# Last turn with transposes by TensorE, and an epilogue with matmuls in TensorE's pauses: a cross-attention and quantized feed-forward kernel on one core

## The chip, the cores and the metric

One Trainium2 chip, one NeuronCore. The metric is the device time of one execution in microseconds (us), the median of several runs. The profile is of one further execution; its times are counted from the start of its span.

## What is computed

Two blocks on x, 32 batches of 100 tokens and 256 features, with a context of 361 tokens per batch. The reference, cut to what matters:

```
x = x + xattn(layernorm(x), ctx, ctx, WQ, WK, WV, WO, mask)
x = x + ffn(layernorm(x), W1, b1, W2, b2)

def xattn(Q, K, V, ...):                     # 16 heads of 64
    logits = Qh @ Kh.T / sqrt(64) + mask * -1e9
    return concat(softmax(logits) @ Vh) @ WO

def ffn(x, ...):                             # 256 -> 1024 -> 256
    h = gelu(qlinear(x, W1, b1))
    return qlinear(h, W2, b2)

def qlinear(x, W, b):
    amin, amax = min(x), max(x)              # over the whole tensor
    scale = max((amax - amin) / 255, 1e-8)
    zp = clip(round(-amin / scale) - 128, -128, 127)
    xq = clip(round(x / scale) + zp, -128, 127)
    wq, sw = symmetric codes of W, -127 .. 127
    return ((xq - zp) @ wq.T) * (scale * sw) + b
```

The range of each quantized input is taken over all batches, so the first matmul of the feed-forward block can't begin before the last batch is through attention, and the second not before every hidden value is known.

## The kernel before, in words

**Stages.** A first stage (to about 105 us) computes the queries of all batches. Then a loop over the batches does attention: one partial turn in front ("first"), 31 turns of a hardware loop ("whole"), one partial turn behind it ("last"), which finishes batch 31 alone. An epilogue follows: the range of the normalized y, its codes, the first matmul with GELU, the range of the hidden values, their codes, the second matmul and the output.

**Float pairs.** Attention is done in pairs of 16-bit floats, a high and a low half. A product of two pairs is three matmuls (`split3`, lines 337 to 343).

**What a turn does for a head.** K, V and QP are the projections and the scores. MAX (VectorE, line 939) reads the scores out of PSUM into `prob` with the row's extreme, EXP (ScalarE, line 711) makes the exponential. The high half of `prob` goes into `hl` by HA on ScalarE (line 717) or, for the heads in VH = 2, 5, 8, 11, 14, by HV on VectorE (line 946). LO on GpSimd (line 585) writes the low half. DT on SP (line 484) transposes the halves of two heads into `pT` with one DMA transpose. PV (TensorE, line 1226) is nine small matmuls per head with the values, into `obank`; a column of ones beside the values gives the sum of each row.

**What it does for a group of four heads.** NORM (VectorE, lines 950 and 953) divides. AH (ScalarE, line 731) and AL (GpSimd, line 589) write the high and low halves into `ahl`. AD on SP (line 488) transposes two groups into `attT` with a DMA transpose. WO (TensorE, twelve matmuls of lines 341 to 343) is one half of the output product, and the same name on VectorE (line 986) adds it to x1, which lies in `q_all`.

**Layer norm of a batch.** LN 0 and 1 (VectorE, lines 998 and 1000) are the moments, RSTD (GpSimd, lines 593 to 597) the factor and shift, YN (ScalarE, line 734) writes y of 100 x 256, LN 2 and 3 (lines 1003, 1005) take its largest and smallest values, LN 4 (line 1007) puts them into `red`. M (line 568) copies a scale.

**Order.** Each engine's order in a turn is computed in `turn` from tables of due times (`PE_STEPS`, `ACT_STEPS`, `DVE_STEPS`, `SP_STEPS`, `POOL_STEPS`), and each engine goes through its list strictly in order. For the last turn `turn` keeps the steps that belong to the current batch. Before the change the lists of the last turn are, for TensorE, PV 6 to 15, WO 0, WO 1; for GpSimd, LO 10 to 15, AL 0, M, AL 1 to 3, RSTD; for ScalarE, HA 7, EXP 11, EXP 12, AH 0, EXP 13, HA 8, EXP 14, HA 9, EXP 15, HA 10, AH 1 to 3, YN (HA 7 to 10 are heads 10, 12, 13 and 15); for VectorE, NORM 1, MAX 15, HV 4 (head 14), NORM 2, NORM 3, WO 0, WO 1, LN 0 to 4; for SP, X, DT 5 to 7, AD 0, AD 1, OUT.

**Buffers.** `pT` and `hl` have 8 places. In PSUM, `proj` are two banks for K, V and WO, `ring` four banks for the scores of four heads, `obank` two for PV.

**Epilogue.** `top_red` (line 1249) transposes `red` by two matmuls, so that each row sees the range over all partitions; `quant_scalars` on VectorE (lines 1023 to 1031) is a chain of eight small steps, each waiting for the one before. `y_codes` (lines 1039 and 1043) and line 767 of ScalarE make codes of y for blocks of four batches; GpSimd makes those of blocks 4 to 7 (lines 632, 634). `y_transposes` (line 1258) transposes a block by eight transposes, sixteen for two blocks, into PSUM; `y_out` copies it out (line 1049 on VectorE for block 0, line 771 on ScalarE for the others). The first matmul (line 1280) does two blocks at once, four matmuls of 400 columns for each of 32 pieces of 128 hidden units, GELU is line 780, and VectorE takes the extremes of each 1600 columns of hidden values (lines 1059, 1060). Then come `top_red(1)`, the scalars again, the hidden codes (line 787 on ScalarE, lines 1078 and 1068 on VectorE) and the second matmul (line 1291), eight matmuls of 256 columns for each of 25 blocks of 128 tokens; block n waits for the codes of its chunk of 400 tokens. Line 1073 adds, and SP writes out.

Of the kernel before, what the change touches and what calls it, by code (L numbers as in the profile page):

```python
# [148 lines left out]
EARLY, LATER = slice(0, 3), slice(3, None)  # L149

S1, INV1, LO1, HI1, S2, INV2, LO2, HI2, SPAN, ZP = range(10)
SW, INVW = 10, 12
# [3 lines left out]
def build(nc, x, ctxT, mask, wq, wk, wv, wo, w1T, b1, w2T, b2, out):  # L156
# [34 lines left out]
    nmax = place("nmax", [P, H], F32)  # L191
    row = place("row", [P, 12], F32)
    red = place("red", [P, 2, 2], F32)
# [127 lines left out]
    s_ad = [sem(f"s_ad{n}") for n in range(2)]  # L321
    s_wp, s_x1 = sem("s_wp"), sem("s_x1")

    s_w12 = [sem("s_w1"), sem("s_w2")]
# [102 lines left out]
    def y_copied(eng, c):  # L427

        eng.wait_ge(*((s_yT, 1) if c == 0 else (s_yTa, c)))

# [19 lines left out]
    def _(sp):  # L450
# [26 lines left out]
        def sp_turn(b, part, steps=slice(None), dummy=False):  # L477
            for kind, n, later in turn(SP_STEPS, part)[steps]:
# [41 lines left out]
    def _(pool):  # L520
# [39 lines left out]
        def pool_turn(b, part, steps=slice(None)):  # L560
            for kind, n, later in turn(POOL_STEPS, part)[steps]:
                a = b + later
# [83 lines left out]
    def _(act):  # L646
# [58 lines left out]
        def act_turn(b, part, steps=slice(None)):  # L705
            banks = bank_of(part)
            for kind, n, later in turn(ACT_STEPS, part)[steps]:
                a, ps = b + later, banks.get((kind, n))
# [19 lines left out]
                elif kind == "AH":  # L728
                    wait(act, s_nrm, NG * a + n + 1)
                    wait(act, s_wp, 2 * a + n // 2 - 1)  # L730
                    act.activation(ahl[0:T, n, 0, :], att[0:T, n % 2, :], ACT.Copy).then_inc(s_ah, 1)  # L731
                elif kind == "YN":
                    wait(act, s_rl, 3 * a + 3)
# [58 lines left out]
    def _(dve):  # L792
# [136 lines left out]
        def dve_turn(b, part):  # L929
            banks = bank_of(part)  # L930
            for kind, n, later in turn(DVE_STEPS, part):
                a, ps = b + later, banks.get((kind, n))
# [9 lines left out]
                elif kind == "HV":  # L942
                    h = VH[n]
                    wait(dve, s_exp, H * a + h + 1)
                    wait(dve, s_pv, H * a + h // 2 * 2 + 1 - RT)
                    dve.tensor_copy(hl[0:T, h % RT, 0, 0:S], prob[0:T, h % RP, 0:S]).then_inc(s_hv, 1)  # L946
                elif kind == "NORM":
                    o = obank[n % 2][0:T, 0:GH * DV].rearrange("p (h d) -> p h d", h=GH)
# [67 lines left out]
        link = chain(dve, s_dve)  # L1016
        wait(dve, s_ln, LN_STEPS * B)
        dve.sem_inc(s_rd, 1)
# [84 lines left out]
    def _(pe):  # L1103
# [69 lines left out]
        def pe_turn(b, part):  # L1173
            jobs, banks = turn(JOBS, part), bank_of(part)

            before = [(kind, n, later - 1) for kind, n, later in turn(JOBS, "whole")[-2:]]
            for kind, n, later in turn(PE_STEPS, part):
                a, ps = b + later, banks.get((kind, n))
# [36 lines left out]
                elif kind == "PV":  # L1215
                    j, half = n // GH, n // HT
                    pe.wait_ge(s_dt[n % RT // 2], 16 * (H // RT * a + n // RT + 1))
                    if n % GH == 0:
# [21 lines left out]
        with pe.Fori(0, B - 1) as b:  # L1240
            pe_turn(b, "whole")
        pe_turn(B - 1, "last")


# [7 lines left out]
        def y_transposes(c):  # L1252
# [7 lines left out]
            ins.then_inc(s_yt, 1)  # L1260

        top_red(0)
        pe.wait_ge(s_wq, 2)
        y_transposes(0)
        y_transposes(1)
        for pair in range(NP2):
            for m in range(NF):
                g = pair * NF + m
                if m == 2 and pair < NP2 - 1:
                    y_transposes(2 * pair + 2)  # L1270
                    y_transposes(2 * pair + 3)
                if m == 0:
                    y_copied(pe, 2 * pair)
                    y_copied(pe, 2 * pair + 1)
                if g >= 3:
                    pe.wait_ge(s_ge, g - 2)
                for k in range(KD):
                    for n in range(2):
                        c = 2 * pair + n
                        ins = pe.matmul(wide[g % 3][:, n, 0:TW], w1q[:, k, m * P:(m + 1) * P],  # L1280
                                        yT[:, k, c * TW:(c + 1) * TW], start=k == 0, stop=k == KD - 1)
                ins.then_inc(s_f1, 1)
        top_red(1)
        pe.wait_ge(s_wq, 4)
        for n in range(NT):
# [39 lines left out]
```

## Time and profile before

| | us |
|---|---|
| runs, median (lowest to highest) | 1129.66 (1129.05 to 1130.61) |
| the profiled execution, its own time | 1126.18 |
| its span | 1124.1 |
| TensorE matmuls busy | 1018.1 (91%) |
| VectorE busy | 978.2 (87%) |
| ScalarE busy | 865.1 (77%) |
| GpSimd busy | 770.6 (69%) |

The shares are means over the span. The loop over the batches covers it from about 105 to 1004 us; the last turn goes from there to about 1028, the first quantized matmul with its ranges to 1094, the second to 1124. In the profile PE is TensorE's matmuls, PEld its weight loads, DVE VectorE, ACT ScalarE, POOL GpSimd, SP the engine that issues DMAs; PEq, DVEq and so on are their sequencers.

### The profile page before, as it was taken

Reading aid. Unit: us, or ns where it says so; the run is one execution under the profiler, and the core shown is the slowest. Engines: PE = TensorE matmul, PEld = TensorE weight load, DVE = VectorE, ACT = ScalarE, POOL = GpSimd, SP = SyncE. Lnnn points to the kernel's source line nnn. Section 1 sums busy time; section 2 is a strip of 40 time slices with the busy share of each in tenths; the row PEclk is TensorE's granted clock in tenths of the full one; section 3 lists DMA queues with packets and bytes.
Section 4 is the critical chain, followed back from the end, with each engine's and each line's share of the span. In section 5 each row is a group of like instructions: output and inputs, shape, how many; then the busy total and the mean of one; then the engine's idle time right before and its main releaser. Section 6 shows DMA issues by size and latency. Waiting matters only on the chain.

```text
span 1124.1 us, 37431 instructions
## 1 busy us (share of the span) xinstructions
PE 1018.1 (91%) x10489; PEld 643.3 (57%) x10489; DVE 978.2 (87%) x2528; ACT 865.1 (77%) x1805; POOL 770.6 (69%) x1108
## 2 busy tenths in 40 slices
PE   3999999999999999999999999999999999985808
PEld 2555566666666666666666666666666666653307
DVE  5777999999999999999999999999999999973997
ACT  4555888888888888888888888888888888873916
POOL 2246877777777777777777777777777777773700
PEclk9999999999999999999999999999999999996969
DMA  8301665555555555555555555555555555555003
GB/s 253 113 1 31 130 134 131 131 135 135 135 135 131 130 135 132 130 131 134 135 135 135 135 135 135 132 130 130 134 135 135 132 130 130 134 132 153 1 0 117
DMA packets 441419, 138.22 MB, mean 123 GB/s; under 512 B 413650, under 2 KB 440374, under 8 KB 441398
## 3 DMA queue, kind: packets, MB, share of 16 engines
q1 hardware_dynamic: 441398, 137.96, 51.0%
q8 instruction: 11, 0.18, 0.1%
q14 instruction: 10, 0.08, 0.0%
HBM read 28.60 MB, written 6.55 MB: 31 GB/s over the span
## 4 chain that ended last, share of the span: by engine, by line
PE 75%; DVE 10%; ACT 5%; issue 4%; POOL 3%; DMA 1%; DVEq 1%; ACTq 0%; SPq 0%; POOLq 0%
PE front L341 19%; PE front L343 17%; PE front L342 17%; PE back L1226 8%; PE front L1208 6%; PE tp L1208 5%; POOL hl L585 3%; DVE hrange L1059 2%; DVE hrange L1060 2%; DVE prob L939 2%; ACT prob L711 2%; DVE k_l L959 1%; ACT q_h L749 1%; PE front L1291 1%; ACT ctx_h L745 1%
## 5 line engine op out<-in xcount | busy, mean ns | idle before, releaser
L585 POOL TENSOR_TENSOR hl<-prob,hl 100x361 f16<-100x361 f32 x512 | 432.1, 853 | 97.2 <-DVE hl L946 50.9
L711 ACT ACTIVATE prob<-prob,nmax 100x361 f32<-100x361 f32 x512 | 293.9, 587 | 47.7 <-DVE nmax L939 47.5
L341 PE MATMUL front<-ctx_h,wk_h 128*128 128x362 f16 x512 | 164.2, 321 | 31.3 <-POOL ctx_l L574 17.8
L1226 PEld LDWEIGHTS back<-v,pT 128*128 128x128 f16 (+1 forms) x4608 | 165.1, 98 | 45.1 <-issue 9.6
L717 ACT ACTIVATE hl<-prob 100x361 f16<-100x361 f32 x352 | 176.0, 500 | 7.9
L1226 PE MATMUL back<-v,pT 128*128 128x65 f16 (+1 forms) x4608 | 174.2, 194 | 6.3 <-DMA pT<-hl 6.2
L343 PE MATMUL front<-ctx_h,wk_l 128*128 128x362 f16 x512 | 161.7, 316 | 0.0
L342 PE MATMUL front<-ctx_l,wk_h 128*128 128x362 f16 x512 | 161.5, 315 | 0.0
L721 ACT ACTIVATE k_h<-front 128x362 f16<-128x362 f32 x256 | 118.9, 464 | 54.7 <-PE front L343 54.7
L959 DVE SCALAR_TENSOR_TENSOR k_l<-front,k_h 128x362 f16<-128x362 f32 x256 | 135.2, 528 | 24.4 <-ACT k_h L721 21.8
L939 DVE CUSTOM_DVE_ANT_0 prob<-front,mask_g,ngain 100x361 f32<-100x361 f32 x256 | 149.6, 584 | 2.2
L965 DVE SCALAR_TENSOR_TENSOR v<-front,v 128x512 f16<-128x512 f32 (+1 forms) x192 | 132.8, 692 | 20.1 <-ACT v L725 17.0
L939 DVE CUSTOM_DVE_ANT_0 prob<-tp,mask_g,ngain 100x361 f32<-100x361 f32 x256 | 147.2, 585 | 3.1
L725 ACT ACTIVATE v<-front 128x512 f16<-128x512 f32 (+1 forms) x192 | 114.3, 596 | 45.9 <-PE front L343 41.8
L341 PE MATMUL front<-wv_h,ctx_h 128*128 128x512 f16 (+1 forms) x384 | 145.9, 380 | 0.0
L342 PE MATMUL front<-wv_l,ctx_h 128*128 128x512 f16 (+1 forms) x384 | 145.5, 379 | 0.0
L343 PE MATMUL front<-wv_h,ctx_l 128*128 128x512 f16 (+1 forms) x384 | 145.5, 379 | 0.0
L946 DVE CAST hl<-prob 100x361 f16<-100x361 f32 x160 | 131.5, 822 | 0.3 <-ACT prob L711 0.3
L589 POOL TENSOR_TENSOR ahl<-att,ahl 100x256 f16<-100x256 f32 x128 | 84.5, 670 | 31.3 <-ACT ahl L731 31.3
L341 PEld LDWEIGHTS front<-ctx_h,wk_h 128*128 128x128 f16 x512 | 49.6, 97 | 88.1 <-DVE k_l L959 27.9
L574 POOL TENSOR_TENSOR ctx_l<-ctx_raw,ctx_h 128x361 f16<-128x361 f32 x64 | 53.1, 853 | 43.9 <-ACT ctx_h L745 43.9
L341 PE MATMUL front<-wo_h,attT 128*100 128x256 f16 x256 | 71.6, 280 | 2.3 <-DMA attT<-ahl 2.3
(180 smaller groups left out, 1980.8 us busy)
## 6 DMA issues: line engine op xcount, KB each, us to landing
ctx_raw<-ctxT SPq DMA_DIRECT2D x33, 361.0 KB, 3.1
pT<-hl SPq DMA_TRANSPOSE x256, 3.1
xs<-x SPq DMA_DIRECT2D x8, 400.0 KB
q_all<-x SPq DMA_DIRECT2D x32, 100.0 KB
out<-q_all SPq DMA_DIRECT2D x32, 100.0 KB
xb<-out SPq DMA_DIRECT2D x5, 640.0 KB, 7.5
out<-xb SPq DMA_DIRECT2D x25, 128.0 KB, 1.8
q_all<-wq SPq DMA_DIRECT2D x1, 1024.0 KB, 6.6
```

The lines of the kernel that those rows point to most:

```text
L341: eng.matmul(dst, lh, rh, start=first, stop=False)
L342: eng.matmul(dst, lh, rl, start=False, stop=False)
L343: return eng.matmul(dst, ll, rh, start=False, stop=final)
L585: pool.tensor_tensor(hl[0:T, n % RT, 1, 0:S], prob[0:T, n % RP, 0:S], hl[0:T, n % RT, 0, 0:S], ALU.subtract).then_inc(s_lo, 1)
L711: act.activation(prob[0:T, n % RP, 0:S], prob[0:T, n % RP, 0:S], ACT.Exp, bias=nmax[0:T, n:n + 1], scale=-1.0).then_inc(s_exp, 1)
L717: act.activation(hl[0:T, h % RT, 0, 0:S], prob[0:T, h % RP, 0:S], ACT.Copy).then_inc(s_ha, 1)
L939: dve.tensor_tensor_reduce(prob[0:T, n % RP, 0:S], ring[n % RP][0:T, 0:S], mask_g[0:T, 0:S], ngain[0:T, 0:1], 3.0e38, ALU.add, ALU.min, nm ...
L946: dve.tensor_copy(hl[0:T, h % RT, 0, 0:S], prob[0:T, h % RP, 0:S]).then_inc(s_hv, 1)
L959: dve.scalar_tensor_tensor(out=k_l[:, n % 4, :], in0=ps[:, 0:SE], scalar=KS, in1=k_h[:, n % 4, :], op0=ALU.mult, op1=ALU.subtract).then_in ...
L965: dve.scalar_tensor_tensor(out=v[:, 1], in0=ps[0:rows_of(n), :].rearrange("p (h d) -> p h d", h=HT), scalar=VS, in1=v[:, 0], op0=ALU.mult, ...
L1208: ins = pe.matmul(ring[(2 * n + h) % RP][:, 0:SE], qs[rows[h], n, :], ks[rows[h], n % 4, :], start=t == 0, stop=t == 2)
L1226: ins = pe.matmul(obank[j % 2][:, n % GH * DV:(n % GH + 1) * DV], pT[0:r, n % RT, part_ * ST + st, :], v2[half][0:r, st, v, n % HT, :], st ...
```

## The change

For the last turn, lists written out by hand take the place of those from the due times. Heads 10 to 15 and all four groups of the last batch are transposed by TensorE (PT, six per head; AT, four per group) into PSUM and copied out (PC, AC) by ScalarE or VectorE, in place of the DMA transposes DT 5 to 7 and AD 0 and 1. Two low halves move from GpSimd to VectorE (DL for head 14, DAL for group 3). Three groups of six matmuls whose results nobody reads (KW) stand between the transposes. The products come in another order (AT 0 before PV 14, AT 1 and WO 0 before AT 2 and 3), and M stands before LO 11. In the last batch the extremes are taken of x1 (LX), and the two of them are scaled and shifted (YM) to give those of y (LM). In the epilogue TensorE does matmuls without a use (`keep_warm`) while it waits, VectorE instead of ScalarE copies block 1 of the transposed codes, and the first piece of the first matmul does block 0 before block 1.

The diff, cut to its core (declarations of semaphores, `row` with two more columns, and the loops' one changed name are left out):

```diff
+LAST_PE = [("PV", n) for n in range(6, 10)] + [
+    ("PT", 10), ("KW", 0), ("PT", 11), ("KW", 1), ("PT", 12), ("KW", 2), ("PT", 13), ("PT", 14), ("PV", 10), ("PV", 11),
+    ("PT", 15), ("PV", 12), ("PV", 13), ("AT", 0), ("PV", 14), ("PV", 15), ("AT", 1), ("WO", 0),
+    ("AT", 2), ("AT", 3), ("WO", 1)]
+LAST_ACT = [
+    ("HA", 7), ("EXP", 11), ("EXP", 12), ("AH", 0), ("EXP", 13), ("HA", 8), ("EXP", 14), ("HA", 9), ("EXP", 15),
+    ("HA", 10), ("PC", 11), ("PC", 13), ("AH", 1), ("AC", 0), ("AH", 2), ("AC", 1), ("AH", 3), ("YM", 0), ("YN", 0)]
+LAST_DVE = [
+    ("NORM", 1), ("MAX", 15), ("HV", 4), ("PC", 10), ("DL", 14), ("PC", 12), ("PC", 14), ("PC", 15),
+    ("NORM", 2), ("NORM", 3), ("DAL", 3), ("AC", 2), ("AC", 3), ("WO", 0), ("WO", 1), ("LN", 0), ("LN", 1),
+    ("LX", 0), ("LX", 1), ("LM", 0), ("LM", 1)]
+LAST_SP = [("X", 0), ("OUT", 0)]
+LAST_POOL = [
+    ("LO", 10), ("M", 0), ("LO", 11), ("LO", 12), ("LO", 13), ("LO", 15), ("AL", 0), ("AL", 1), ("AL", 2), ("RSTD", 0)]
...
+    last_bank = {n: (proj[n % 2] if n < 12 else ring[n % RP]).bitcast(F16) for n in range(10, H)}
+    att_bank = [ring[n].bitcast(F16) for n in range(NG)]
...
-        eng.wait_ge(*((s_yT, 1) if c == 0 else (s_yTa, c)))
+        eng.wait_ge(*((s_yT, c + 1) if c < 2 else (s_yTa, c - 1)))
...
+                elif kind == "PC":
+                    act.wait_ge(s_pt, n - 9)
+                    wait(act, s_pv, H * a + n + 1 - RT)
+                    act.activation(pT[:, n % RT, :, 0:T],
+                                   last_bank[n][:, 0:2 * ST * T].rearrange("p (c t) -> p c t", c=2 * ST),
+                                   ACT.Copy).then_inc(s_pca, 1)
...
+                elif kind == "YM":
+                    wait(act, s_rl, 3 * a + 3)
+                    wait(act, s_ln, LN_STEPS * a + 4)
+                    act.activation(row[0:T, 12:14], row[0:T, 10:12], ACT.Identity, scale=row[0:T, 9:10],
+                                   bias=row[0:T, 8:9]).then_inc(s_ym, 1)
...
-        y_out(1)
         act.wait_ge(s_yd, 2)
...
+                elif kind == "DL":
+                    wait(dve, s_hv, len(VH) * a + VH.index(n) + 1)
+                    dve.tensor_tensor(hl[0:T, n % RT, 1, 0:S], prob[0:T, n % RP, 0:S], hl[0:T, n % RT, 0, 0:S],
+                                      ALU.subtract).then_inc(s_dl, 1)
...
+                elif kind == "LX":
+                    wait(dve, s_x1, 2 * a + 2)
+                    dve.tensor_reduce(row[0:T, 10 + n:11 + n], x1_slot(a), AX.X, (ALU.max, ALU.min)[n]).then_inc(s_ln, 1)
...
         y_out(0)
+        y_out(1)
         y_codes(2)
...
+                elif kind == "PT":
+                    if n < 12:
+                        wait(pe, s_v, 2 * ST * (a + 1))
+                    if n == 14:
+                        pe.wait_ge(s_dl, 1)
+                    else:
+                        wait(pe, s_lo, H * a + n + 1 - int(n > 14))
+                    for c in range(2 * ST):
+                        ins = pe.transpose(last_bank[n][:, c * T:(c + 1) * T],
+                                           hl[0:T, n % RT, c // ST, c % ST * P:(c % ST + 1) * P], identb[0:T, 0:T])
+                    ins.then_inc(s_pt, 1)
+                elif kind == "KW":
+                    for _ in range(6):
+                        pe.matmul(obank[0][:, 512 - P:512], w1q[:, 0, 0:P], w1q[:, 0, 0:P], start=True, stop=True)
+                elif kind == "AT":
+                    if n == 3:
+                        pe.wait_ge(s_dal, 1)
+                    else:
+                        wait(pe, s_al, NG * a + n + 1)
+                    pe.wait_ge(*((s_pcd, 2), (s_pca, 2), (s_pcd, 3), (s_pcd, 4))[n])
+                    for c in range(4):
+                        ins = pe.transpose(att_bank[n][:, c * T:(c + 1) * T],
+                                           ahl[0:T, n, c // 2, c % 2 * P:(c % 2 + 1) * P], identb[0:T, 0:T])
+                    ins.then_inc(s_at, 1)
                 elif kind == "WO":
-                    pe.wait_ge(s_ad[n], 16 * (a + 1))
+                    if part != "last":
+                        pe.wait_ge(s_ad[n], 16 * (a + 1))
+                    else:
+                        pe.wait_ge((s_aca, s_acd)[n], 2)
...
+        pe.wait_ge(s_wq, 2)
         pe_turn(B - 1, "last")
...
+        def keep_warm(times, dst):
+
+            for _ in range(times):
+                pe.matmul(dst, w1q[:, 0, 0:P], w1q[:, 0, 0:D], start=True, stop=True)
+
+        for n in (1, 2, 4):
+            wait(pe, s_ln, LN_STEPS * (B - 1) + n)
+            keep_warm(6, obank[1][:, 0:D])
         top_red(0)
-        pe.wait_ge(s_wq, 2)
+        for n in range(1, 9, 2):
+            pe.wait_ge(s_dve, n)
+            keep_warm(3, obank[1][:, 0:D])
+        pe.wait_ge(s_yd, 1)
+        keep_warm(3, obank[1][:, 0:D])
         y_transposes(0)
         y_transposes(1)
...
+                by_chunk = [(k, n) for n in range(2) for k in range(KD)]
+                for k, n in by_chunk if g == 0 else sorted(by_chunk):
...
+        pe.wait_ge(s_hx, 2 * NP2 * NQ - 4)
+        keep_warm(32, tp[1][:, 0:D])
         top_red(1)
+        for n in range(9, 17, 2):
+            pe.wait_ge(s_dve, n)
+            keep_warm(3, tp[1][:, 0:D])
+        pe.wait_ge(s_hd, 1)
+        keep_warm(3, tp[1][:, 0:D])
         pe.wait_ge(s_wq, 4)
```

AC and DAL are written like PC and DL, on 400 and 256 columns; PC 11 and 13 and AC 0 and 1 are ScalarE's, the others VectorE's, and PV of heads 10 to 15 waits for the copy of its head.

## Rows read from the trace of the kernel before

**Rows 1.** The page: the chain that ended last, by engine.

```profile
PE 75%; DVE 10%; ACT 5%; issue 4%; POOL 3%; DMA 1%; DVEq 1%; ACTq 0%; SPq 0%; POOLq 0%
```

**Rows 2.** Busy time by stretches; the column after POOL is TensorE's granted clock.

```profile
1008.70:1018.90 10.20, 6.14 (x66) 5.30 (x66) 1.50 (x5) 1.91 (x5) 5.02 (x8) 0.50 0.59 125
1018.90:1025.70 6.80, 1.48 (x12) 1.26 (x12) 1.30 (x4) 0.26 (x1) 1.05 (x3) 1.00 0.20 49
1025.70:1039.40 13.70, 7.52 (x47) 4.78 (x48) 7.31 (x19) 7.93 (x9) 7.12 (x6) 0.50 0.75 241
...
1073.50:1100.80 27.30, 3.41 (x15) 2.25 (x16) 24.73 (x26) 5.34 (x3) 0.00 (x0) 0.50 0.00 0
1100.80:1124.10 23.30, 20.61 (x189) 18.22 (x186) 18.77 (x33) 13.41 (x5) 0.00 (x0) 1.00 0.42 141
```

**Rows 3.** The chain in order of time, last turn and first matmul: start, us, what.

```profile
1010.09 0.84 POOL hl L585
...
1011.08 3.66 DMA pT<-hl
...
1014.79 1.19 PE back L1226 x18
...
1016.22 0.44 DVE att L953
...
1016.67 0.42 ACT ahl L731
...
1018.10 2.62 DMA attT<-ahl
...
1020.85 0.28 PE front L341
...
1022.37 0.49 DVE q_all L986
...
1034.06 2.83 PE front L1280 x8
```

**Rows 4.** Timeline of the last turn: start, us, engine, line, operation.

```profile
1005.99 0.73 PE L1226 MATMUL back<-v,pT 128*128 128x65 f16 x18 [0.48 <-DMA pT<-hl]
...
1008.26 0.35 DVE L946 CAST hl<-prob 100x361 f16<-100x361 f32 x1
...
1009.00 0.51 ACT L717 ACTIVATE hl<-prob 100x361 f16<-100x361 f32 x1
```

**Rows 5.** Line 946 over the whole span: durations in ns, shortest, median, longest.

```profile
L946 DVE CAST hl<-prob x160: 340/671/1856, 106.9 to 1008.3; 100x361 f16<-100x361 f32 x160
```

**Rows 6.** The chain in order of time, from YN to the range's transposes.

```profile
1025.44 0.61 ACT q_all L734
...
1027.49 0.70 PE tp L1249 x2
```

**Rows 7.** Timeline: ScalarE's smallest instruction of that stretch.

```profile
1027.35 0.20 ACT L764 ACTIVATE rinv<-rinv 100x1 f32<-100x1 f32 x1
```

**Rows 8.** Timeline of the codes and the first matmul.

```profile
1031.55 1.49 PE L1258 MATMUL tp<-identb,y 100*128 100x100 f16 x16 [3.38 <-DVE y L1043]
...
1032.41 0.57 DVE L1049 COPY yT<-tp 128x800 f16<-128x800 f16 x1 [0.48 <-PE tp L1258]
...
1033.08 0.84 ACT L771 ACTIVATE yT<-tp 128x800 f16<-128x800 f16 x1 [0.60 <-PE tp L1258]
...
1035.67 1.02 ACT L780 ACTIVATE q_all<-front,b1c,sc 128x800 f32<-128x800 f32 x1 [1.76 <-PE front L1280]
...
1037.98 1.82 DVE L1059 TENSOR_REDUCE hrange<-q_all 128x1 f32<-128x1600 f32 x1 [4.08 <-ACT q_all L780]
...
1046.44 0.87 PE L1258 MATMUL tp<-identb,y 100*128 100x100 f16 x16
```

**Rows 9.** Timeline of the second matmul's start.

```profile
1098.08 4.99 PE L1291 MATMUL front<-w2q,hq 128*128 128x256 f16 x32 [3.69 <-DVE hq L1068]
...
1102.91 1.11 DVE L1068 TENSOR_SCALAR hq<-hq,sc 128x3200 f16<-128x3200 int16 x1
```

More of the change, by code:

```diff
@@ L149, with order @@
 EARLY, LATER = slice(0, 3), slice(3, None)
+LAST_PE = [("PV", n) for n in range(6, 10)] + [
[6 more added lines that the diff above has]
+LAST_DVE = [
[3 rows of a table added]
+LAST_SP = [("X", 0), ("OUT", 0)]
+LAST_POOL = [
+    ("LO", 10), ("M", 0), ("LO", 11), ("LO", 12), ("LO", 13), ("LO", 15), ("AL", 0), ("AL", 1), ("AL", 2), ("RSTD", 0)]
+def order(events, part, last):
+    return [(kind, n, 0) for kind, n in last] if part == "last" else turn(events, part)
 S1, INV1, LO1, HI1, S2, INV2, LO2, HI2, SPAN, ZP = range(10)
@@ L191, in build @@
     nmax = place("nmax", [P, H], F32)
-    row = place("row", [P, 12], F32)
+    row = place("row", [P, 14], F32)
     red = place("red", [P, 2, 2], F32)
@@ L322, in build @@
     s_wp, s_x1 = sem("s_wp"), sem("s_x1")
+    s_dl, s_dal, s_pt, s_at = sem("s_dl"), sem("s_dal"), sem("s_pt"), sem("s_at")
+    s_pca, s_pcd, s_aca, s_acd, s_ym = sem("s_pca"), sem("s_pcd"), sem("s_aca"), sem("s_acd"), sem("s_ym")
     s_w12 = [sem("s_w1"), sem("s_w2")]
@@ L477, in sp_turn @@
         def sp_turn(b, part, steps=slice(None), dummy=False):
-            for kind, n, later in turn(SP_STEPS, part)[steps]:
+            for kind, n, later in order(SP_STEPS, part, LAST_SP)[steps]:
                 a = b + later
@@ L560, in pool_turn @@
         def pool_turn(b, part, steps=slice(None)):
-            for kind, n, later in turn(POOL_STEPS, part)[steps]:
+            for kind, n, later in order(POOL_STEPS, part, LAST_POOL)[steps]:
                 a = b + later
@@ L706, in act_turn @@
             banks = bank_of(part)
-            for kind, n, later in turn(ACT_STEPS, part)[steps]:
+            for kind, n, later in order(ACT_STEPS, part, LAST_ACT)[steps]:
                 a, ps = b + later, banks.get((kind, n))
@@ L731, in act_turn @@
                     act.activation(ahl[0:T, n, 0, :], att[0:T, n % 2, :], ACT.Copy).then_inc(s_ah, 1)
+                elif kind == "PC":
[4 more added lines that the diff above has]
+                                   ACT.Copy).then_inc(s_pca, 1)
+                elif kind == "AC":
+                    act.wait_ge(s_at, n + 1)
+                    wait(act, s_wp, 2 * a)
+                    act.activation(attT[:, n, :, 0:T], att_bank[n][:, 0:4 * T].rearrange("p (c t) -> p c t", c=4),
+                                   ACT.Copy).then_inc(s_aca, 1)
+                elif kind == "YM":
[3 more added lines that the diff above has]
+                                   bias=row[0:T, 8:9]).then_inc(s_ym, 1)
                 elif kind == "YN":
@@ L930, in dve_turn @@
             banks = bank_of(part)
-            for kind, n, later in turn(DVE_STEPS, part):
+            for kind, n, later in order(DVE_STEPS, part, LAST_DVE):
                 a, ps = b + later, banks.get((kind, n))
@@ L946, in dve_turn @@
                     dve.tensor_copy(hl[0:T, h % RT, 0, 0:S], prob[0:T, h % RP, 0:S]).then_inc(s_hv, 1)
+                elif kind == "DL":
+                    wait(dve, s_hv, len(VH) * a + VH.index(n) + 1)
+                    dve.tensor_tensor(hl[0:T, n % RT, 1, 0:S], prob[0:T, n % RP, 0:S], hl[0:T, n % RT, 0, 0:S],
+                                      ALU.subtract).then_inc(s_dl, 1)
+                elif kind == "DAL":
+                    wait(dve, s_ah, NG * a + n + 1)
+                    dve.tensor_tensor(ahl[0:T, n, 1, :], att[0:T, n % 2, :], ahl[0:T, n, 0, :],
+                                      ALU.subtract).then_inc(s_dal, 1)
+                elif kind == "PC":
+                    dve.wait_ge(s_pt, n - 9)
+                    wait(dve, s_pv, H * a + n + 1 - RT)
+                    dve.tensor_copy(pT[:, n % RT, :, 0:T],
+                                    last_bank[n][:, 0:2 * ST * T].rearrange("p (c t) -> p c t", c=2 * ST)).then_inc(s_pcd, 1)
+                elif kind == "AC":
+                    dve.wait_ge(s_at, n + 1)
+                    wait(dve, s_wp, 2 * a)
+                    dve.tensor_copy(attT[:, n, :, 0:T],
+                                    att_bank[n][:, 0:4 * T].rearrange("p (c t) -> p c t", c=4)).then_inc(s_acd, 1)
+                elif kind == "LX":
+                    wait(dve, s_x1, 2 * a + 2)
+                    dve.tensor_reduce(row[0:T, 10 + n:11 + n], x1_slot(a), AX.X, (ALU.max, ALU.min)[n]).then_inc(s_ln, 1)
+                elif kind == "LM":
+                    dve.wait_ge(s_ym, 1)
+                    if n == 0:
+                        ins = dve.tensor_tensor(red[0:T, 0, 0:1], red[0:T, 0, 0:1], row[0:T, 12:13], ALU.max)
+                    else:
+                        ins = dve.scalar_tensor_tensor(out=red[0:T, 0, 1:2], in0=row[0:T, 13:14], scalar=-1.0,
+                                                       in1=red[0:T, 0, 1:2], op0=ALU.mult, op1=ALU.max)
+                    ins.then_inc(s_ln, 1)
                 elif kind == "NORM":
@@ L1016, in _ @@
         link = chain(dve, s_dve)
-        wait(dve, s_ln, LN_STEPS * B)
+        wait(dve, s_ln, LN_STEPS * B + 1)
         dve.sem_inc(s_rd, 1)
@@ L1176, in pe_turn @@
             before = [(kind, n, later - 1) for kind, n, later in turn(JOBS, "whole")[-2:]]
-            for kind, n, later in turn(PE_STEPS, part):
+            for kind, n, later in order(PE_STEPS, part, LAST_PE):
                 a, ps = b + later, banks.get((kind, n))
@@ L1216, in pe_turn @@
                     j, half = n // GH, n // HT
-                    pe.wait_ge(s_dt[n % RT // 2], 16 * (H // RT * a + n // RT + 1))
+                    if part != "last" or n < 10:
+                        pe.wait_ge(s_dt[n % RT // 2], 16 * (H // RT * a + n // RT + 1))
+                    else:
+                        copied = [m for kind_, m in (LAST_ACT if n in (11, 13) else LAST_DVE) if kind_ == "PC"]
+                        pe.wait_ge(s_pca if n in (11, 13) else s_pcd, copied.index(n) + 1)
                     if n % GH == 0:
@@ L1273, in _ @@
                     y_copied(pe, 2 * pair)
+                if m == 0 and pair > 0:
                     y_copied(pe, 2 * pair + 1)
@@ L1276, in _ @@
                     pe.wait_ge(s_ge, g - 2)
[L1277 to L1281, printed above, removed]
+                by_chunk = [(k, n) for n in range(2) for k in range(KD)]
+                for k, n in by_chunk if g == 0 else sorted(by_chunk):
+                    c = 2 * pair + n
+                    if g == 0 and k == 0 and n == 1:
+                        y_copied(pe, 1)
+                    ins = pe.matmul(wide[g % 3][:, n, 0:TW], w1q[:, k, m * P:(m + 1) * P],
+                                    yT[:, k, c * TW:(c + 1) * TW], start=k == 0, stop=k == KD - 1)
                 ins.then_inc(s_f1, 1)
+        pe.wait_ge(s_hx, 2 * NP2 * NQ - 4)
+        keep_warm(32, tp[1][:, 0:D])
         top_red(1)
+        for n in range(9, 17, 2):
[3 more added lines that the diff above has]
+        keep_warm(3, tp[1][:, 0:D])
         pe.wait_ge(s_wq, 4)
```

2 lines of the change are left out of this document (added).

## The prediction

> **What bounds the kernel now.** I read the chain of waits over the whole span first, then the clock by stretches, then the chain in order of time from 1003 us on, and last the timeline of the same stretch. The chain belongs to TensorE for three quarters of the span [rows 1], and those are the 31 turns of the loop over the batches, which the change leaves as they are. All that it edits runs once: the last turn and the two quantized matmuls behind it, from about 1004 us to 1124 us. There the chain is another one. It runs over GpSimd's last low half (LO 15, until 1010.93), a DMA transpose of 3.66 us, the products of heads 14 and 15, NORM, AH and AL of the last group, a DMA transpose of 2.62 us, and twelve matmuls of WO 1 that end in the addition at 1022.37 to 1022.86 [rows 3]. TensorE stops at 1006.72 [rows 4] and has its next products only when transposes land; its clock is at 1.2 GHz from 1008.7 to 1018.9, from 1025.7 to 1039.4, and from 1073.5 to 1100.8 [rows 2]; each time it fell behind a stretch in which TensorE stood idle, and rose behind a dense one.
>
> **Time base.** The profiled execution took 1126.18 us, span 1124.1, and the median of the runs is 1129.66, which is 3.48 above it. I work out differences in the profiled execution and take them from the median.
>
> **Last turn: transposes by TensorE.** Six transposes per head (heads 10 to 15) replace three DMA transposes, four per group replace two, and each needs a copy out of PSUM. SP's queue loses five issues (DT 5 to 7, AD 0 and 1) and keeps X and OUT, which wait for what they waited for. TensorE's wait for the codes of the first weights moves ahead of this turn; they are made before the loop, so it costs nothing. Prices: sixteen y transposes take 0.87 us at 2.4 GHz and 1.49 at 1.2 [rows 8], so six take about 0.4 or 0.65 and four 0.3 or 0.4, with the drain. A copy of 800 columns takes 0.57 on VectorE and 0.84 on ScalarE [rows 8]; 600 columns (PC) scale to about 0.45 and 0.67, 400 (AC) to 0.35 and 0.5. The products of a head take 0.73/2 = 0.37 at 2.4 GHz [rows 4], 1.19/2 = 0.6 at 1.2 [rows 3]. Followed through the new orders:
> - GpSimd does LO 10, M, LO 11, 12, 13 as before (M, formerly after AL 0, lies in the gap ahead of LO 11), no LO 14, and LO 15 when HA 10 has ended at 1009.51 [rows 4]: with the hop, 9.65 to 10.5 (all times from here to the end of this list are less 1000), where it ended at 10.93.
> - VectorE ends HV 4 at 8.61 [rows 4]; PC 10 until 9.1, the low half DL 14, PC 12 until 10.1, PC 14 until 10.8, PC 15 at 11.4 to 11.85. ScalarE: PC 11 until 10.2, PC 13 until 10.9, AH 1 until 11.35.
> - TensorE: PT 10 at 6.75, then PT 11 to 13 each right behind its LO, with the six idle matmuls KW in between (0.35 a group, and the gaps are as long), PT 14 until 10.2, PV 10 and 11 until 10.95, PT 15 until 11.35, PV 12, PV 13, AT 0 until 12.25, PV 14 and 15 until 13.05, AT 1.
> - Tail: AC 0 until 12.9, AH 2, AC 1 until 13.85 on ScalarE; WO 0 at 14.0, twelve matmuls in 1.5 us (from 1020.85 to 1022.37) [rows 3]; AT 2 and AT 3 behind it until 15.9 (NORM 3 took 0.69 from the end of PV 15 to AH 3, AH 3 0.42, and DAL 3 is priced like NORM's multiplication of as many columns, 0.44 [rows 3]: over at 14.8, with the wait for AC 1, and not late); AC 2 and 3 until 16.4; WO 1 from 16.55 to 18.05; addition until 18.6.
> That is 4.3 us ahead of the 22.86 of before. I take off 0.3 for eight new hand-overs between engines that no row shows: **4.0**.
>
> Unknown here is DL 14, a subtraction of 361 columns with both sources in SBUF, beside a running GpSimd. From below it is the 0.35 of a bare cast, from above the longest cast of the same tile beside GpSimd, 1.86 [rows 5]; I take 0.5, as the last cast beside GpSimd took 0.35 [rows 4]. At 1.86 it moves PT 14 and PC 14 by 1.3, of which PT 15's wait on LO 15 hides 0.6: 0.7 lost. The Trainium skill (SBUF — State Buffer, section "SBUF: two separate sides") has such an instruction and a reading GpSimd instruction shut each other out for a whole instruction; by that, DL 14 would wait some 0.2 for LO 13 and push LO 15 back by 0.2, and the sum would be 0.2 smaller. The casts' spread [rows 5] agrees with that.
>
> **Layer norm's range.** The largest and smallest of y are now taken of x1 (LX 0, LX 1), while GpSimd works on the root, and two numbers are scaled instead of 256. The stretch from YN to the transposes of the range took 1027.49 - 1025.44 = 2.05 [rows 6]. It becomes a small activation (0.20 [rows 7]), two small VectorE steps of at most as much, and three hops: 0.7. **1.35** gained. The full YN (0.61) runs behind the small one; then the table load, needed before the first codes, still ends ahead of them by about 0.1. In TensorE's queue the three batches of six keep-warm matmuls of 256 columns stand before the transposes; at 2.4 GHz one takes 20.61/189 = 0.109 [rows 2], a batch 0.65, and the last is over 0.6 before the range is ready. They cost nothing then. At 1.2 GHz the eighteen take 3.84 and end 1.2 after it: this term is then near 0.15.
>
> **Codes and first matmul.** At 2.4 GHz the transposes of the range take about 0.45 for 0.70 [rows 6]: **0.25**. The batches of three (0.33) at every second step of the scalar chain fit between two waits of 0.4. Sixteen y transposes are 0.6 shorter, VectorE copies both blocks (its second copy is 0.57 in place of ScalarE's 0.84, but queued behind the first, and y_codes 2 and 3 behind both, 1.2 before they are needed), the first two matmuls need only block 0, and eight matmuls that took 2.83 [rows 3] take 1.4. By the steps: copy 0 ends 0.3 earlier, copy 1 at 33.2 for 33.9, the first GELU starts at 33.9 in place of 35.67, and the range of piece 0 at 35.95 in place of 37.98 [rows 8]. With the 0.1 that the second piece had to wait for: **2.1**. From there VectorE's 32 reductions of 1.73 set the time as before; nothing done to TensorE in them counts. GpSimd's codes of blocks 4 to 7 and its weights move along with the scalars and have 10 us and more in hand.
>
> **Second matmul.** Thirty-two matmuls start when four reductions (6.9 us) are left; at 1.2 GHz all of them would take 6.8, so they are over before the transposes need the engine. With the clock up, 0.25 comes from the range's transposes, and the first 32 matmuls take 3.5 for 4.99 [rows 9]. But block 6 waits for the codes of chunk 2, until 1102.91 + 1.11 [rows 9], and starts at 1104.15 at the earliest, for 1104.82: **0.25 + 0.65 = 0.9**. From there TensorE is busy to the end.
>
> Sum: 4.0 + 1.35 + 0.25 + 2.1 + 0.9 = 8.6, so 1129.66 - 8.6 = **1121.0 us**.
>
> **The rivals.**
> (a) *The clock falls in the last turn.* For it: heads 10 to 13 give TensorE only transposes and 18 short matmuls over 3 us; a clock that reacts to that falls about as it did [rows 2]. From PT 14 on at 1.2 GHz, PV 10 to 15 take 0.6 each, a head's transposes 0.65, WO 0 2.65, and WO 1 ends at 22.0 even if the clock is back for it: this term shrinks from 4.0 to 0.4, and the time is 1124.6. Against it: no gap is longer than 0.7, where before TensorE stopped at 1006.72 and was idle for 10.2 - 6.14 = 4.1 of the 10.2 us at 1.2 GHz [rows 2, 4]. The Trainium skill (TensorE: Matmul & The Clock Gate, "Part 4: PE-mode transpose") says that transposes do not engage the full clock as other matmuls do, which is this rival. By that, the trace agrees to a point: sixteen transposes from 1031.55 ran at 1.2 GHz, but so did the eight dense matmuls behind them [rows 2, 3, 8]. Chance 0.17.
> (b) *The 32 matmuls end too soon* and the clock is down again at the second range: the last term is 0, 1121.9. Chance 0.13.
> (c) *Slower: TensorE becomes the last turn's bound, at 1.2 GHz throughout.* From 1006.72 on: six PT (3.7), three KW (1.9), six PV (3.6), four AT (1.6), WO 0 and WO 1 (5.2), with hand-overs in the tail of 1.6, is 17.6: WO 1 ends at 24.3, 1.95 later than before. The keep-warm batches leave 0.15 of the layer norm's gain and cost 0.35 before the y transposes; the earlier start on block 0 still brings 0.95. In all 1.95 - 0.15 + 0.35 - 0.95 = +1.2, 1130.9. It decides if the clock is down before about 1008 and stays. Against it: TensorE comes from the loop at 2.4 GHz and stands still for under 0.7. Chance 0.05.
> (d) *The removed DMA transposes were hidden*: they would be if something else released WO 1, but the chain passes through both and TensorE waits for them by name. No change: chance 0.03.
> My forecast: 0.62, with DL 14 and hand-overs anywhere within their bounds.
>
> **How the numbers follow.** The forecast's own range is 1120.0 (no cost for hand-overs, 0.3 of spread between runs) to 1122.3 (DL 14 at its upper end, hand-overs doubled). (b) lies in it. To leave out no more than 2 in 10 the range has to take in (a) in most of its size: 1119.6 to 1125.2. A difference of 0.2% (2.3 us) is about what a measurement of this kernel can tell. Forecast, (a) and (b) are all faster by more: 0.62 + 0.17 + 0.13, of which I take 0.04 for what I have overlooked, 0.88. (c) and (d) give mostly no change, 0.08, and 0.04 is left for slower.
>
> **What would show it.** Right: no DMA transposes after those of heads 8 and 9; TensorE without a gap over 1 us from 1007 to 1018 and with a clock of 1.00 in it; WO 1 over at about 1018; range transposes about 3.3 us behind the last addition instead of 4.6; the first reduction of piece 0 7.6 us earlier than before (about 1030.4); 55 us of reductions unchanged; clock 1.00 from the first matmul of the second layer. Wrong: 0.50 between 1009 and 1018 (a), 0.50 at the second layer's first block (b), a keep-warm matmul that ends behind the DVE step it sits beside (c), LO 15 or PT 14 over 1 us late (DL 14).

## The result, and the profile after

The changed kernel takes 1116.73 us (median of 4 runs, 1116.15 to 1118.23) beside 1129.36 (4 runs, 1128.42 to 1130.61) of the kernel before in the same measurement: ratio 0.9897, 95% interval 0.9883 to 0.9911. That is 12.6 us faster, and below the range that I gave. Repeated in experiment 5 it was 0.9894 (0.9877 to 0.9910). The profiled execution took 1116.15 us, its span 1114.3; against the profiled execution of before that is 10.0 less. So two things have to be told apart: what the two profiles show, 10.0 for the 8.6 that I forecast, and 2.6 that they don't show (of before, the profiled execution lies 3.2 below its median; of the changed kernel, 0.6).

The chain in order of time of the changed kernel: the products of heads 4 to 7, with which I begin to count, the way from the low half of head 13 to the first reduction (start, us, what; x1 is complete behind `q_all L1055`), and its end:

```profile
1004.07 1.22 PE back L1300 x36
...
1008.27 0.84 POOL hl L610
1009.15 0.44 PE front L1311 x6
1009.59 0.39 PE tp L1311 x6
1009.98 0.55 PE back L1300 x18
1010.53 0.27 PE tp L1311 x6
1010.80 0.55 PE back L1300 x18
1011.35 0.19 PE front L1324 x4
...
1011.97 0.41 ACT ahl L756
1012.37 0.44 ACT attT L766
...
1012.95 0.28 PE front L366
...
1016.95 0.50 DVE q_all L1055
...
1020.03 0.40 ACT row L771
...
1020.79 0.45 PE tp L1351 x2
...
1024.52 0.54 PE tp L1360 x8
1025.08 0.58 DVE yT L1118
1025.71 1.01 PE front L1397 x4
1026.83 1.94 ACT q_all L820 x2
1028.79 1.82 DVE hrange L1129
...
1082.39 1.74 DVE hrange L1130
...
1091.70 1.05 PE front L1415 x8
...
1111.33 0.48 DVE xb L1143
```

These answer to [rows 3, 6, 8, 9] and to these pieces of the chain before:

```profile
1004.30 1.22 PE back L1226 x36
...
1091.70 1.74 DVE hrange L1060
...
1121.45 0.48 DVE xb L1073
```

The two DMA transposes have left the chain; it goes through TensorE, with short copies. WO 0 starts at 1012.95, before at 1015.81. Stage by stage, profile against profile: the loop came 0.22 earlier. From the products of heads 4 to 7 to x1's last addition 5.19 is saved (12.88 for 18.07). From x1 to the range's transposes it took 3.34 for 4.63, 1.29 saved, and the transposes 0.45 for 0.70, 0.25. From their end to the first reduction 7.55 for 9.79, 2.24, and 0.11 less behind the first two reductions. From the last reduction to the last output's addition 27.20 for 28.01, 0.81. The end of the span lies 0.3 later behind that addition. Sum 9.8, and 0.2 outside the span.

Busy time by stretches of the changed kernel (columns as in [rows 2], the granted clock behind POOL):

```profile
1004.10:1017.50 13.40, 10.46 (x202) 9.26 (x201) 9.50 (x30) 7.43 (x16) 6.30 (x9) 1.00 0.16 38
1017.50:1028.80 11.30, 8.85 (x81) 5.62 (x82) 6.85 (x23) 7.41 (x9) 4.74 (x6) 1.00 0.75 243
1028.80:1063.50 34.70, 24.44 (x148) 10.79 (x146) 34.70 (x21) 31.77 (x36) 24.60 (x15) 1.00 0.06 19
1063.50:1080.20 16.70, 2.93 (x14) 2.10 (x15) 16.70 (x10) 0.00 (x0) 0.00 (x0) 0.50 0.00 0
1080.20:1114.30 34.10, 27.19 (x237) 22.30 (x234) 27.41 (x49) 18.75 (x7) 0.00 (x0) 1.00 0.29 97
```

The clock stays at 2.4 GHz through the last turn and the first matmul. It is down only while VectorE reduces, and up again before the second range.

### The profile page after: what moved, and what is told of

Its sections match the earlier page's. It is cut to its first block, busy times and chain, and to the rows that moved or that the text cites. A ratio compares the mean times of both kernels' runs of the same rounds, so it can differ in the third digit from the quotient of the medians.

```text
span 1114.3 us, 37739 instructions
## 1 busy us (share of the span) xinstructions
PE 1026.3 (92%) x10639; PEld 649.0 (58%) x10639; DVE 982.0 (88%) x2538; ACT 866.6 (78%) x1809; POOL 770.5 (69%) x1106
## 4 chain that ended last, share of the span: by engine, by line
PE 75%; DVE 10%; ACT 6%; issue 4%; POOL 3%; DVEq 1%; DMA 1%; ACTq 1%; SPq 0%; POOLq 0%
PE front L366 19%; PE front L368 17%; PE front L367 17%; PE back L1300 8%; PE front L1278 6%; PE tp L1278 5%; POOL hl L610 3%; DVE hrange L1129 2%; DVE hrange L1130 2%; DVE prob L979 2%; ACT prob L736 2%; DVE k_l L1028 1%; ACT q_h L790 1%; ACT ctx_h L786 1%; PE front L1415 1%
```

## The experiments

**1. The kernel before, again.** Nothing edited.

> The kernel before, unchanged, for its spread. The change brought 12.6 us of median where the two profiled executions differ by 10.0, because the profiled execution of before (1126.2) lies 3.2 below the median of its runs. Theory A (clock): TensorE's clock falls and rises in the pauses of the last turn and of the epilogue, and where it does differs from execution to execution; the profiled execution was a favourable one. Then the executions of this kernel spread over 1126 to 1131 us, the longer ones show the lower mean clock (0.970 to 0.977), and a new profile differs from the old one behind 1004 us only. Theory B (loop or frame): the 3 us lie in the loop or outside the span. Then the mean clock is the same 0.977 in all executions, or the profiles differ ahead of 1004 us.

Ratio 1.0001 (0.9991 to 1.0012), 1125.73 to 1129.72 in 12 runs. Each run has its mean granted clock, and over 51 executions of the kernel before in all experiments (three chips) the times go by it:

| mean clock | executions | us, lowest to highest | mean |
|---|---|---|---|
| 0.977 | 12 | 1125.35 to 1126.95 | 1125.9 |
| 0.976 | 18 | 1126.89 to 1129.28 | 1128.4 |
| 0.974 | 8 | 1127.57 to 1128.78 | 1128.1 |
| 0.973 | 13 | 1128.29 to 1130.27 | 1129.0 |

The execution on whose profile I built the forecast has 0.977 and 1126.18, so it is one of the quick quarter. The new profile is of one with 0.976 and 1128.11; a stretch of it, and the chain from the products of heads 4 to 7 to WO 1:

```profile
1010.90:1024.20 13.30, 8.88 (x78) 7.66 (x78) 1.70 (x5) 0.83 (x2) 3.42 (x6) 0.50 0.41 87
```

```profile
1004.88 1.22 PE back L1226 x36
...
1015.37 1.19 PE back L1226 x18
...
1018.68 2.62 DMA attT<-ahl
...
1021.44 0.42 PE front L341
1021.86 0.21 PE front L342
...
1024.00 0.23 PE front L343
1024.25 0.50 DVE q_all L986
```

Here WO 1 runs at 1.2 GHz, a matmul every 0.21 us, from 1021.44 to 1024.25: 2.8 us, where [rows 3] have 1.5. From the products of heads 4 to 7 to x1's last addition this execution takes 1.3 longer (19.37 for 18.07), all of it there; the other 0.6 of its longer span lie ahead of the last turn, where nothing is edited. That 0.6 is a spread of its own: in the fourteen profiles here the products of heads 4 to 7 begin anywhere from 1003.99 to 1005.89. So for the last turn Theory A holds (the profile of kernel 4 below has the same slow WO 1), and for a smaller part Theory B. What the executions at 0.973 pay for beyond this, no profile of mine shows.

**2 to 4. The change in halves.** Kernel 2 is the changed kernel without its idle matmuls. Kernel 3 has only the last turn's lists, kernel 4 only the keep-warm matmuls, VectorE's second copy and the order of the first matmul. The diffs of the experiments are cut to the lines that matter.

```diff
# kernel 2
-    ("PT", 10), ("KW", 0), ("PT", 11), ("KW", 1), ("PT", 12), ("KW", 2), ("PT", 13),
+    ("PT", 10), ("PT", 11), ("PT", 12), ("PT", 13),
...
         def keep_warm(times, dst):
+            return
```

```diff
# kernel 3, against the changed kernel
-    ("LX", 0), ("LX", 1), ("LM", 0), ("LM", 1)]
+    ("LN", 2), ("LN", 3), ("LN", 4)]
...
         def keep_warm(times, dst):
+            return
...
-        y_out(1)                       # VectorE
+        y_out(1)                       # ScalarE, as before
-                for k, n in by_chunk if g == 0 else sorted(by_chunk):
+                for k, n in sorted(by_chunk):
```

> The changed kernel without any matmul that has no use (no KW, no keep-warm; all else as in it). If the clock is what they buy: A says slower than the changed kernel's 1116.7 by 3 to 6 us (1120 to 1123), with clock 0.5 in the epilogue from about 1020 to 1030 us and at the second matmul's start. My forecast's terms give: 0.25 + 0.9 of the clock at the second matmul, about 1.2 of the 2.1 in the codes and the first matmul, nothing in the last turn as long as its clock stays up: 1119. Rival: the clock does not react to them, 1116.7.

> The last turn's new lists with the transposes and KW; layer norm's range, the first matmul and the epilogue as before, no keep-warm. My forecast gave the last turn 4.0, its trace shows 5.2; if terms add up this is 1129.4 - 5.2 = 1124.2. Theory A adds what the unfavourable clock cost before in the last turn (up to 2.6): 1121.6 to 1124.2. Theory B: 1124.2 or more.

> The kernel before with the keep-warm matmuls and the new order of the first matmul alone (old last turn with DMA transposes, old range of y). By the terms of the trace: 0.25 + 2.2 + 0.1 and 0.8 is 3.4, so 1126.0. Theory A: if the 2.6 that the profile did not show lie in the epilogue, 1123.4; if they lie in the last turn, 1126.0 or a little more, since the first eighteen keep-warm matmuls can run at 1.2 GHz here and delay the transposes of the range by up to 1.2.

Measured: kernel 2 1119.45, ratio 0.9927 (0.9912 to 0.9942); kernel 3 1122.23, 0.9947 (0.9931 to 0.9963); kernel 4 1124.98, 0.9971 (0.9961 to 0.9981), beside 1128.29. The last turn alone is worth 6.1 us of median where the two profiles have 5.2. Its interval (4.2 to 7.8) holds both, so that the old turn's slow executions are what it takes away is likely, not shown. The twelve executions of kernel 4, which keeps the old last turn, still fall in two kinds: three at 1122.3 to 1123.2 with a mean clock of 0.985 to 0.988, nine at 1124.7 to 1126.3 with 0.980 to 0.986; the five of kernel 3 lie within 2.1 us. Kernel 4's profile is of the slower kind, with WO 1 at 1.2 GHz from 1021.67 to 1024.48. There the keep-warm matmuls behind it run at 1.2 GHz too, and the range's transposes start 5.09 behind the addition's end, where they started 4.63 behind it. With the 3.3 of kernel 4 and the 1.3 of the layer norm's range the halves come to 10.7 of about 12; the rest is within these intervals. Kernel 2 (mean clock 0.982) lies as my own terms gave it (1119) and below Theory A's 1120 to 1123.

**5 to 7. KW.** Kernel 5 is the changed kernel again, as base; 6 has no KW; 7 has the eighteen KW matmuls as transposes.

```diff
# kernel 7
-                        pe.matmul(obank[0][:, 512 - P:512], w1q[:, 0, 0:P], w1q[:, 0, 0:P], start=True, stop=True)
+                        pe.transpose(obank[0].bitcast(F16)[:, 1024 - P:1024], w1q[:, 0, 0:P], identb[:, :])
```

> The changed kernel, unchanged, for its spread and as the base of the next. Theory A (the clock's fall and rise in pauses costs before a different amount in each execution, and the change takes the pauses away): mean clock 0.991 or 0.992 in every execution, a spread of under 2.5 us, against 0.973 to 0.977 and 4.6 us of the kernel before; median 1116 to 1117.5.

> The changed kernel without the three KW groups in the last turn; keep-warm in the epilogue stays. In the kernel without any idle matmul the clock fell to 0.66 of 1008 to 1011 us and its last turn ended about 1 us later than the changed kernel's. If that is KW's absence: 0.5 to 1.5 us slower than the changed kernel, most of it as PT and PV at 1.2 GHz. Rival: clock 1.00 all through the turn, no difference, as my forecast's sum had it (KW at no gain and no cost).

> The changed kernel with the eighteen KW matmuls as eighteen transposes of the same 128 x 128 tile. If transposes do not hold the clock (rival (a) of the prediction and the page's rule): as the kernel without KW, 0.5 to 1.5 us slower, clock under 1.00 between 1008 and 1014. If a transpose counts as any matmul of its columns: no difference, clock 1.00.

Kernel 5: 1116.69 (1115.25 to 1117.05), clock 0.991 or 0.992 in every execution. Kernel 6: 1118.45, ratio 0.9912 (0.9896 to 0.9928), 1.8 slower; the intervals overlap a little, but each of its five executions is slower than each of kernel 5's. Kernel 7: 1116.45, 0.9894 (0.9876 to 0.9912), as kernel 5. Stretches of kernels 6 and 7, counted in both from the same point of the last turn:

```profile
1005.90:1011.90 6.00, 4.00 (x93) 3.36 (x94) 5.58 (x20) 5.17 (x11) 4.14 (x6) 1.00 0.34 83
1011.90:1015.40 3.50, 3.50 (x65) 3.50 (x61) 1.41 (x5) 1.43 (x4) 1.51 (x4) 0.51 0.01 2
```

```profile
1005.10:1011.10 6.00, 4.99 (x111) 4.30 (x112) 5.59 (x20) 5.17 (x11) 4.15 (x6) 1.00 0.34 83
1011.10:1014.60 3.50, 2.82 (x71) 2.69 (x68) 2.34 (x7) 2.28 (x6) 2.15 (x4) 1.00 0.03 7
```

Without KW TensorE stands for up to 0.7 us between the transposes of heads 10 to 13, and behind them the clock falls to 1.2 GHz; in the 3.5 us that follow it is busy without a pause, the bound of the turn. Products and transposes in that order (timeline of kernel 6, two heads a row):

```profile
1011.62 0.90 PE L1300 MATMUL back<-v,pT 128*128 128x65 f16 x18
...
1012.82 1.19 PE L1300 MATMUL back<-v,pT 128*128 128x65 f16 x18
```

Kernel 6 takes 14.40 from the products of heads 4 to 7 to x1's last addition, the changed kernel 12.88. The 1.5 between them are rival (a) of the prediction in small. With KW as transposes the clock stays at 1.00, and the same way takes 12.87. Eighteen transposes hold the clock here as well as eighteen matmuls of the same size. The Trainium skill (TensorE: Matmul & The Clock Gate, "Part 4: PE-mode transpose") says that the full clock does not engage for transposes; for holding a clock that is up, the measurement decides against it. Whether transposes alone can raise it, no run here shows.

**8. No keep-warm at the end**, and **9. none around the first range.**

```diff
# kernel 8
-        keep_warm(32, tp[1][:, 0:D])
...
-            keep_warm(3, tp[1][:, 0:D])
```

```diff
# kernel 9
-            keep_warm(6, obank[1][:, 0:D])
...
-            keep_warm(3, obank[1][:, 0:D])
```

> The changed kernel without the 32 and the later threes before the second matmul. The forecast's term: 0.25 for the range's transposes and 0.65 behind block 6, 0.9 slower than the changed kernel (measured between its trace and the trace of before: 0.8). Where the clock comes back later than in that profile it costs more, up to 1.3. Range transposes 0.70 instead of 0.45, first 32 matmuls 5.0 instead of 4.0 with their waits.

> The changed kernel without the keep-warm matmuls before and after the first range's transposes; KW and those at the end stay. By the trace without any idle matmul, the transposes of the range still run at 2.4 GHz, the y transposes and the first eight matmuls at 1.2: 0.9 to 1.3 us slower than the changed kernel (the forecast's clock share of its 2.1). Rival: those matmuls delay the chain as much as they help it, no difference.

Kernel 8: 1118.22, ratio 0.9914 (0.9898 to 0.9930), 1.5 slower. Kernel 9: 1118.28, 0.9913 (0.9897 to 0.9930), 1.6 slower; here kernel 5's 1116.69 of another chip is the base. From kernel 8's chain:

```profile
1084.51 0.67 PE tp L1351 x2
...
1088.87 6.20 PE front L1412 x32
```

The first 32 matmuls take 6.20 where the kernel before had 4.99 [rows 9] and 5.04 in its second profile: those caught an early return of the clock, this one a late one. From the last reduction to the last addition it is 29.3 for 27.2, so in this execution the matmuls without a use are worth 2.1. From kernel 9's chain:

```profile
1021.54 0.67 PE tp L1351 x2
...
1025.57 1.49 PE tp L1360 x16
1027.06 2.86 PE front L1395 x8
1029.95 1.03 ACT q_all L820
1031.00 1.82 DVE hrange L1129
```

All three at 1.2 GHz, and the first reduction 13.39 behind the start of x1's last addition instead of 11.84. The expectation missed that the range's transposes slow down too. It came from kernel 2's trace, where they ran at 2.4 GHz without any keep-warm:

```profile
1022.14 0.42 PE tp L1351 x2
```

So the clock lasts from WO 1 to them in one execution and not in the other, and an expectation from one trace of it was a guess. Kernels 6, 8 and 9 lose 1.8, 1.5 and 1.6; together (kernel 2) the loss is 2.7, or 3.7 by the ratios. Their profiles show which parts give it back in these executions. Apart, the last turn loses 1.5, the way from x1 to the first reduction 1.55 and the end 2.1. In kernel 2 they lose 1.35, 0.95 and 1.1 (28.30 for 27.20). There the first range's transposes were quick, and the second matmul's first 32 took 5.21 instead of 6.20.

**10. The order of the first matmul**, and **11. the low half of head 14.**

```diff
# kernel 10
-        y_out(1)                       # VectorE
+        y_out(1)                       # ScalarE
-                for k, n in by_chunk if g == 0 else sorted(by_chunk):
+                for k, n in sorted(by_chunk):
```

```diff
# kernel 11
-    ("LO", 10), ("M", 0), ("LO", 11), ("LO", 12), ("LO", 13), ("LO", 15),
+    ("LO", 10), ("M", 0), ("LO", 11), ("LO", 12), ("LO", 13), ("LO", 14), ("LO", 15),
...
-    ("PC", 10), ("DL", 14), ("PC", 12),
+    ("PC", 10), ("PC", 12),
```

> The changed kernel with the second copy of y codes on ScalarE and the first piece in the old order, all at 2.4 GHz. The first GELU has to wait for ScalarE's 0.84 us copy of block 1 and then for four matmuls (0.85) instead of VectorE's copy and two: 0.3 to 0.6 us slower than the changed kernel. Rival: nothing, because the second piece of the first matmul comes at the same time and the reductions wait for two GELUs.

> The changed kernel with the low half of head 14 back on GpSimd (DL 14 as LO 14, before LO 15). GpSimd's LO 14 takes 0.83 and ends at about 1009.95 where DL 14 took 0.80 until 1009.48 on VectorE; LO 15 then ends at about 1010.8 instead of 1010.3. The chain of the last turn passes LO 15 or the PV behind it: 0.4 to 0.6 us slower. Rival (the subtraction on VectorE is shut out by GpSimd and costs LO 15 as much): no difference.

Kernel 10: 1117.64, ratio 0.9912 (0.9895 to 0.9929), 0.9 slower than kernel 5, with intervals that overlap; in the profiles 0.64 lies between YM and the first reduction (9.40 for 8.76). Kernel 11: 1117.12, 0.9901 (0.9884 to 0.9917), which the runs don't tell apart from the changed kernel, but the profile has the step: 13.31 from the products of heads 4 to 7 to x1's last addition for 12.88, 0.4 as expected. DL 14 itself, in the changed kernel, beside GpSimd's LO 13 and LO 15:

```profile
1008.27 0.83 POOL L610 TENSOR_TENSOR hl<-prob,hl 100x361 f16<-100x361 f32 x1
1008.68 0.80 DVE L989 TENSOR_TENSOR hl<-prob,hl 100x361 f16<-100x361 f32 x1
...
1009.47 0.83 POOL L610 TENSOR_TENSOR hl<-prob,hl 100x361 f16<-100x361 f32 x1 [0.38 <-ACT hl L742]
```

It took 0.80, where I had 0.5, and ended when LO 15 began. Nothing waited for it. DAL 3, the same subtraction on 256 columns beside an idle GpSimd, took 0.43 in this trace; that scales to 0.6 at most for DL 14's 361 columns (an estimate), so some 0.2 of the 0.80 come from LO 13 beside it. No run separates them.

**12. Codes by GpSimd.** Beyond the change, for TensorE's pause at the second matmul.

```diff
+        pool.wait_ge(s_dve, 12)
+        pool.tensor_scalar(hq[:, :, TW + TW // 2:2 * TW].bitcast(I16), hid[:, 1, :, TW // 2:TW],
+                           sc[:, INV2:INV2 + 1], 1.0, ALU.mult, ALU.mult).then_inc(s_hp, 1)
...
-            ts = slice(0, TW // 2 if c == 0 else TW)
+            ts = slice(0, TW // 2 if c <= 1 else TW)
```

> A step beyond the change: at the second matmul TensorE stands twice for the codes of chunks 1 and 2 (about 0.4 us at 1091.3 in the changed kernel, less at 1094.3), which ScalarE's row of codes sets. Here GpSimd, idle there, makes the integers of half of chunk 1. If it runs beside the others, h_codes 1 is 1.4 us earlier, TensorE has no gap from its first to its last matmul, and the whole is 0.6 to 0.9 us faster than the changed kernel. Rival: GpSimd and VectorE shut each other out while VectorE makes the first block's codes, and the start of the second matmul moves by up to 1.7 us: 0.5 to 1.5 us slower.

Kernel 12 takes 1116.31 (1115.92 to 1116.63), ratio 0.9897 (0.9880 to 0.9913); it is not told apart from the changed kernel. Its chain shows why, the expectation and its rival being both right at once:

```profile
1087.24 1.70 DVE hq L1151
1088.94 0.61 DVE hq L1141
...
1089.69 3.65 PE front L1420 x32
1093.34 1.75 PE back L1420 x16
```

VectorE's first integers take 1.70 beside GpSimd's, in the changed kernel 1.05, so the matmul starts 0.65 later; then TensorE has no pause until its last matmul. From the last reduction it is 27.07 for 27.20.

## Why the prediction was wrong

**The step that failed is the time base.** I took differences in one profiled execution and subtracted them from the median of the others. The text itself had the 3.48 us between the two and went on. They were no frame around the span: the 51 executions go by their mean granted clock, the profiled one is of the quick quarter, and the clock in TensorE's pauses is what the change works on. The favourable profile had WO 1 at 2.4 GHz; the two other profiles of the old last turn have it at 1.2 (experiments 1 and 4), which is 1.3 us, and the change takes away the pauses ahead of it. That is half of the 2.6 by which the median falls more than the profiles differ. The place of the other half stays open: a late return of the clock at the second matmul (6.20 or 6.47 us for the first 32 in kernels 8 and 3, for 4.99) would be of that size, but no profile of the kernel before caught one. With this step right and the sizes as I had them the forecast would have been 1118.5, still below my range, and with the sizes right and this step as it was 1119.7, just in it. So this is the step that put the result outside.

**The last turn was mis-sized**, 4.0 for 5.2. Its mechanism, the way of the chain and the clock at 1.00 were right. LO 15 began at 1009.47 (9.69 with the loop's 0.22; forecast 9.65) and WO 0 ran from 1012.95 to WO 1's end in 3.98 (forecast 4.05). Between them I was 0.9 long: two heads' products take 0.55 from start to start and six transposes 0.27, and I had charged each with the time until its last matmul has ended, 0.37 a head and 0.4 for six. Then I took 0.3 off for hand-overs on top, which cost nothing that wasn't in the steps: 4.0 + 0.9 + 0.3 is the 5.2 measured.

**DL 14** took 0.80 for my 0.5, inside the bounds, and was hidden as reckoned; LO 15 was not pushed back by it.

**Layer norm's range**: 1.29 for 1.35, and its transposes 0.25 for 0.25. The keep-warm batches cost nothing in the queue.

**Codes and first matmul**: 2.24 + 0.11 for 2.1. **Second matmul**: 0.81 for 0.9 in the profiles, but experiment 8 puts the part at 1.5 in the median, and its own profile at 2.1. The two profiles of the kernel before have an early return of the clock there; how often it is late in that kernel, they don't show.

**The rivals.** (a) and (c) did not come; without KW a small (a) does (experiment 6), so KW, which I had entered as neither cost nor gain, is worth 1.5 in the profiles and 1.8 in the medians. (b): the 32 matmuls end at 1082.4, two microseconds before the range's transposes, and the clock is still up. (d): the DMA transposes were not hidden.

**Two sums of the prediction are off.** The lower end of the forecast's own range is 1121.0 less 0.3 and 0.3, 1120.4 and not 1120.0; and six PT at 0.65 in (c) are 3.9, not 3.7. Neither moves the forecast.

## What to carry to other kernels

When the profiled execution is 3 us off the median and the change is to give 9, ask first what they are. The mean granted clock that stands beside each run tells whether the clock has a part in them, and which kind of execution the profile is of; in which stage it lies takes a second profile, of an execution of the other kind. Here the kernel whose clock fell in its pauses had a spread of 4.9 us over 51 executions and the changed one 1.8 and 2.1 over five and four, and taking the pauses away gained more than the one favourable trace showed. And add up a stream of short matmuls by their start-to-start times; the end of the last one is paid once, where another engine waits.

## What the runs showed of the hardware

Eighteen matmuls with no use (about 1 us of TensorE in pauses that were there anyway) are worth 1.5 us in the profiles and 1.8 in the medians, and as transposes they do the same. The clock returned at different places behind the same kind of pause: 32 equal matmuls behind a pause took 4.99 [rows 9], 5.04, 5.21, 6.20 and 6.47 us in five executions (before, experiments 1, 2, 8 and 3), all without keep-warm at that place; the first two are of the same program. The same two transposes of the first range took 0.42 (kernel 2) and 0.67 (kernel 9), both without keep-warm ahead of them. VectorE's conversion of 1600 columns to integers took 1.70 beside the same conversion by GpSimd, instead of 1.05 (experiment 12).
